# Head mixing attention: a block's values made behind the scores two tiles on, and VectorE's copy of the outputs behind the next maxima and running sum

## What is computed

```python
attn = jnp.einsum('bhnd,bhmd->bhnm', q, k) * scale
attn = jax.nn.softmax(attn, axis=-1)
attn = jnp.einsum('gh,bhnm->bgnm', conv_w, attn) + conv_b[None, :, None, None]
mean = attn.mean(axis=(0, 2, 3), keepdims=True)
var = attn.var(axis=(0, 2, 3), keepdims=True)
attn = (attn - mean) * jax.lax.rsqrt(var + BN_EPS)
attn = attn * bn_gamma[None, :, None, None] + bn_beta[None, :, None, None]
out = jnp.einsum('bhnm,bhmd->bhnd', attn, v)
```

## Time and profile before

| | |
|---|---|
| median of 3 runs | 4358.7 us (4358.68 to 4359.67) |
| the profiled execution's own time | 4354.42 us |
| its span, first to last instruction | 4352.6 us |
| busy over the span: TensorE, VectorE, ScalarE, GpSimd | 87%, 64%, 51%, 19% |
| busy in one block of 35.15 us in the middle of the stage: TensorE, VectorE, ScalarE, GpSimd | 34.07, 30.58, 26.15, 6.84 us |
| share of the chain that ended last that lies in this stage's lines | none of the lines listed |

### The profile page before, as it was taken

One profiled execution on the slowest core, in us unless ns is written; L12 is line 12 of the kernel. 1 busy time (PEld: TensorE's weight loads), 2 busy tenths in 40 slices (PEclk: granted clock), 3 DMA queues, 4 the chain that ended last, 5 costly groups with the idle time before them and its releaser, 6 DMA issues. The chain is left out here.

```text
span 4352.6 us, 155594 instructions
## 1 busy us (share of the span) xinstructions
PE 3782.2 (87%) x64620; PEld 2304.4 (53%) x64621; DVE 2787.5 (64%) x5455; ACT 2209.1 (51%) x4201; POOL 825.7 (19%) x2119
## 2 busy tenths in 40 slices
PE   5779999799799997688889759999999999966996
PEld 2357777444477774345555425445545545434763
DVE  5546666311566664578788658878878878863343
ACT  1235555311455552466666527767767767721221
POOL 0000000000000000355555401111111111105023
PEclk7879999899899997899999879999999999988997
DMA  1011111100011111000000021000000000023233
GB/s 52 10 32 48 48 51 50 35 0 0 26 48 48 51 49 62 1 1 1 1 1 1 1 74 35 0 1 1 0 1 1 0 1 0 0 90 116 64 92 113
DMA packets 84608, 131.16 MB, mean 30 GB/s; under 512 B 11440, under 2 KB 67024, under 8 KB 83408
## 3 DMA queue, kind: packets, MB, share of 16 engines
q1 hardware_dynamic: 78288, 111.95, 7.7%
q0 software_dynamic: 6144, 16.79, 1.2%
HBM read 69.98 MB, written 58.72 MB: 30 GB/s over the span
## 5 line engine op out<-in xcount | busy, mean ns | idle before, releaser
L1969 PE MATMUL psum<-hm_ex,hm_mix 128*128 128x512 f32 x1024 | 503.0, 614 | 38.8 <-ACT hm_Aq L2065 38.8
L2051 ACT ACTIVATE hm_ex<-psum,hm_nm 128x1024 f32<-128x1024 f32 x256 | 286.0, 1117 | 255.5 <-DVE hm_nm L2123 255.3
L1969 PEld LDWEIGHTS psum<-hm_ex,hm_mix 128*128 128x128 f32 x1024 | 173.9, 189 | 344.8 <-issue 336.9
L2138 DVE COPY hm_A<-psum 128x1024 f32<-128x1024 f32 x256 | 312.7, 1222 | 54.0 <-PE psum L1978 50.3
L2133 DVE TENSOR_SCALAR_CACHE_REDUCE hm_plus<-hm_Aq,hm_cbcol,hm_sums 128x1024 f32<-128x1024 f32 x256 | 340.3, 1329 | 0.0
L2123 DVE TENSOR_REDUCE hm_nm<-psum 128x1 f32<-128x1024 f32 x256 | 310.7, 1214 | 32.2 <-PE psum L1957 32.2
L1978 PEld LDWEIGHTS psum<-K,hm_Aq 128*128 128x128 f32 x2048 | 236.7, 141 | 149.4 <-issue 139.7
L1529 ACT ACTIVATE pt_signs<-pt_acts,pt_tb 128x1024 f32<-128x1024 f32 (+1 forms) x224 | 227.6, 1018 | 116.0 <-POOL pt_tb L1399 94.9
L2056 ACT ACTIVATE hm_junk<-hm_Aq 128x1024 f32<-128x1024 f32 x256 | 270.6, 1057 | 30.3
L1957 PE MATMUL psum<-hm_kt,hm_qd 64*32 64x512 f32 x4096 | 277.9, 601 | 3.2 <-ACT hm_kt L2074 3.2
L1978 PE MATMUL psum<-K,hm_Aq 128*128 128x128 f32 x2048 | 267.3, 273 | 5.6 <-DVE hm_A L2138 5.6
(11 more groups left out here) (415 smaller groups left out, 7949.7 us busy)
## 6 DMA issues: line engine op xcount, KB each, us to landing
fw_late<-fw_away SPq DMA_DIRECT2D x64, 384.0 KB, 3.1
ex_rows_in<-hm_zero SPq DMA_DIRECT2D x2, 5120.0 KB, 24.2
ex_xs<-ex_rows_in SPq DMA_DIRECT2D x80, 128.0 KB, 2.0
ex_rows_out<-ex_ys SPq DMA_DIRECT2D x80, 128.0 KB, 1.7
fw_away<-fw_kk SPq DMA_DIRECT2D x64, 128.0 KB, 1.8
fw_away<-fw_tr SPq DMA_DIRECT2D x64, 128.0 KB, 1.7
fw_away<-fw_qm SPq DMA_DIRECT2D x64, 128.0 KB, 1.7
ex_w<-in_ex_w SPq DMA_DIRECT2D x2, 4096.0 KB, 19.6
```

Of the source, the lines that this page charges most:

```text
L1969: mm = pe.matmul(bank[4 + c], mix[:, u, :], ex[:, u, 512 * c:512 * c + 512], start=True, stop=True)
L2051: act.activation(ex[:, u, :], flat2(psum[:, 2 * u:2 * u + 2, :]), ACT.Exp, bias=nm[:, u:u + 1], accum_out=rsum[:, u:u + 1]).then_inc(s_ex, 1)
L2138: dve.tensor_copy(A[:, :, :, QT_ * t:QT_ * t + QT_], flat2(psum[:, 6:8, :]).rearrange("p (m g n) -> p m g n", m=MT, g=HEADS)).then_inc(s_a ...
```

## The change

In every block but a batch's first, at tiles 1 and 2:

- TensorE, tile 1: `scores` of tile 3 goes ahead of `values`, and `turn` of tile 0, which closed tile 1, leaves it.
- TensorE, tile 2: after `mixed` of 2 come the wait for `outputs`, `turn` of 0, `scores` of 4 and `turn` of 1 (before: `turn` of 1, `scores` of 4).
- VectorE, tile 1: `maxima` of 3 and `running` of 1 go ahead of `outputs` and `evacuate` of 0; tile 2 is left with `inverse` of 3 and `evacuate` of 1.

No instruction is added or removed, and no buffer changes.

```diff
                             mixed(i, t % 2, more)
                             if t == 0 and not first:
                                 turn(i - 1, 1)
+                            if t > 2 or t == 2 and first:
+                                turn(i - 1, (t - 1) % 2)
+                            if t == 2 and not first:
+                                pe.wait_ge(s_pv_ev, b * NB * 2 + n * 2 + 2)
+                                turn(i - 2, 0)
+                            if more:
+                                scores(i + 2, t % 2)
+                            if t == 1 and first:
+                                pe.wait_ge(s_v_ev, b * 2 + 2)
+                                turn(i - 1, 0, free=False)
                             if t == 1 and not first:
                                 values(n - 1)
-                            if t > 1:
-                                turn(i - 1, (t - 1) % 2)
-                            if more:
-                                scores(i + 2, t % 2)
-                            if t == 1:
-                                if first:
-                                    pe.wait_ge(s_v_ev, b * 2 + 2)
-                                else:
-                                    pe.wait_ge(s_pv_ev, b * NB * 2 + n * 2 + 2)
-                                turn(i - 1, 0, free=not first)
+                            if t == 2 and not first:
+                                turn(i - 1, 1)
...
                             more = not (last and t == NQ - 1 or first and t == 0)
-                            if more:
+                            early = t == 2 and not first
+                            if more and not early:
                                 maxima(i + 1, (t + 1) % 2)
-                            if not (first and t == 0):
+                            if not (first and t == 0) and not early:
                                 running(i - 1, (t - 1) % 2)
                             if more:
                                 inverse(i + 1, (t + 1) % 2)
                             if t == 1 and not first:
+                                maxima(i + 2, t % 2)
+                                running(i, t % 2)
                                 outputs(n - 1)
                             if not (first and t == 0):
                                 evacuate(i - 1, (t - 1) % NQ)
```

## The result

| | before | the change |
|---|---|---|
| median | 4359.48 us (12 runs, 4352.26 to 4370.03) | 4377.89 us (12 runs, 4367.28 to 4384.18) |
| ratio | | 1.0033, interval 1.0025 to 1.0041 |
| span of the profiled execution | 4352.6 us | 4376.4 us |
| a block in the middle of the stage | 35.15 us | 35.59 us |

A forecast was written before the change was run, and what follows sets the result against it. TensorE was taken to set the pace, standing 1.08 us a block; a new chain of waits adds 0.38 us at each of 28 boundaries, 10.6 us, to 4358.7, giving 4369.3 us. Range 4358 to 4380 us, the forecast's own 4363 to 4376.

The forecast's parts named there:

- the three cases: Whole program against a 0.2% threshold: slower by more 0.61, faster by more 0.10, between 0.29.
- rival 3: Boundary: longer `mixed` of 2 (1.91) and bank release (1.52) cost 0.7 us each, 19.6 us in all, 4378 us; chance 0.09.
- the forecast's chain: Boundary, banks 6 and 7: linked waits from `mixed` of 1 bring `mixed` of 4 at 2737.95 instead of 2737.55, 0.40 us later.
- What bounds: Within a block TensorE sets the pace, 3.81 us a tile; its only stand is 1.08 us ahead of `mixed` of 3.
- rival 1: Boundary: early maxima free `keep`, nothing replaces the 1.08 us wait; 30.2 us faster, 4328.5 us; chance 0.09.
- What goes: Boundary: `maxima` of 3 and `running` of 1 fit VectorE's 2.92 us idle gap, ending the old reason for the 1.08 us.
- The two waits: TensorE at a boundary: about 0.5 us ahead of `turn` of 1 and 1.0 us ahead of `mixed` of 4.
- VectorE's four gaps: Idle at a boundary: 0.3 ahead of `maxima`, 1.2 of `outputs`, 2.1 of `evacuate` of 0, 1.15 of `evacuate` of 1.
- the signs of being wrong: `mixed` of 4 under 16.1 us behind `mixed` of 1, a block's tile pace other than 3.81 us, or TensorE clock below 1.00.
- `mixed` of 2 to `turn` of 0: TensorE at a boundary, start to start: 1.76 us taken, from 1.72 or 1.79 in the trace, bound 1.91.
- The sum: All 28 boundaries at 0.38 us each: 10.6 us slower; batch ends, first blocks and other stages cost nothing more.
- Rival 2: Within the block: the delay is caught up over five tiles, no measurable change, 4354 to 4364 us; chance 0.22.

The follow-up runs named there:

- the last experiment: Kernel before, only `maxima` of 3 moved on VectorE, behind `outputs` and ahead of `evacuate` of 0 at every boundary; TensorE's order unchanged: ratio 0.9929.
- TensorE's half alone: TensorE's order as in the change, VectorE's as in the kernel before: ratio 1.021.
- VectorE's half alone: VectorE's order as in the change, TensorE's as in the kernel before: ratio 1.0227, from two runs.
- with `turn` of 0 back: Against the change: wait for `outputs` and `turn` of 0 back ahead of `mixed` of 2, `turn` of 1 ahead of `scores` of 4; VectorE as changed: ratio 0.9984.

## Why the prediction was right

The measured median, 4377.89 us, lies in the range, near its upper end; slower by over 0.2% was the likeliest of the three cases and came. It lies outside the forecast's own 4363 to 4376 us, though, and right at rival 3's 4378: by the time alone rival 3 would have come. That the forecast's chain is what happened is told by the trace, with 0.44 us a boundary and not 0.7. By its steps:

- **What bounds.** Right. TensorE stood 1.08 us a block, and nothing else could be gained: the version that removes exactly that reaches 34.10 us and the 30 us that rival 1 had reckoned for it.
- **What goes.** Right as to `maxima` of 3 (2735.28, 0.23 us behind the reciprocal), its `exponentials` and the early `keep` of 2, released by `turn` of 0.
- **The chain.** Right in every link, most of them to 0.02 us: 1.91, 1.02, 3.63, then 1.82, 1.08, 1.37, 1.10, 1.14, 1.25, 1.11 and 1.15. Together 16.58 us from `mixed` of 1 to `mixed` of 4, where I had 16.52 and the kernel before has 16.12. The two waits are 0.39 and 1.08 us where I had 0.5 and 1.0, and VectorE's four gaps 0.23, 1.23, 2.15 and 1.18 where I had 0.3, 1.2, 2.1 and 1.15. Of the signs of being wrong none came at a boundary; a clock below 1.00 came once, at the stage's last `values`.
- **The term that was mis-sized** is `mixed` of 2 to `turn` of 0: 1.76 taken, 1.82 measured, just outside the 1.72 and 1.79 between which I chose, though inside the bound of 1.91. The weight loads of that `mixed` started with its first matmul, at 2738.73 for both, and not ahead of it:

```profile
2738.73 0.30 PEld L1970 LDWEIGHTS psum<-hm_ex,hm_mix 128*128 128x128 f32 x2 [0.20 <-issue]
```

The Trainium skill's rule of weight loads pulled ahead (TensorE: Matmul & The Clock Gate, the table of facts at its head) is not what happened at this place, although `weights` of tile 2 had long been done; by it the sum would have been 0.34 us a boundary, by the trace it is 0.44. The trace of before had held the right figure: in its ordinary tiles, where `mixed` follows `scores`, the first weights start with the matmul and `turn` comes 1.83 us behind.

```profile
2737.55 1.98 PE L1969 MATMUL psum<-hm_ex,hm_mix 128*128 128x512 f32 x4
2739.38 1.04 PE L1978 MATMUL psum<-K,hm_Aq 128*128 128x128 f32 x8
```
```profile
2737.55 0.30 PEld L1969 LDWEIGHTS psum<-hm_ex,hm_mix 128*128 128x128 f32 x2 [0.84 <-issue]
```
- **The sum.** 28 x 0.38 = 10.6 us forecast; 28 x 0.44 = 12.3 us in the trace; 14.4 us by the ratio, whose interval of 10.9 to 17.9 holds 12.3. The remaining 1.3 us that the profiled stage is longer is the clock at its last `values`, to which the prediction ("the batch ends ... cost nothing more") gave nothing. Whether the change brought that fall is open: each kernel has one profile. My point of 4369.3 us is 8.6 below the median, of which the chain explains 1.7; the rest is within what runs of one kernel differ by.
- **Rival 1** (faster, the wait goes and nothing replaces it) did not come, for the reason given. Its price was right, and its place was one step away: with `maxima` of 4 taken forward too it is at 34.47 us, with TensorE left alone at 34.10. What I had written under it as needed was too little: since a boundary starts from a loss of 0.40 us, half of the gain (0.54) asks for a chain shorter by 0.94 us and not by 0.7, and all of it for 1.48 and not 1.0.
- **Rival 2** (caught up within the block) did not come: behind the wait the tiles take 3.78 us (2748.75 to 2752.53) and no less. **Rival 3** (0.7 us a boundary) did not either.
- The advice of the Trainium skill that rival 1 names (Perfetto Trace Analysis, Optimization Strategy: find the gap and make what it waits for start sooner) agrees with the last experiment (34.10 us a block) and not with the change (35.59). Both make the same maxima sooner; they differ in what they make later.

## What to carry to other kernels

When a step is moved forward on an in-order engine to end a wait, follow the next instance of the same step too: it may now be queued behind something that waits longer, and the old wait comes back one tile on. An idle gap on a helping engine is best filled with just what the bound engine waits for and what fits the gap; here one 1.2 us step moved gained 31 us, while moving two steps there and reordering three on TensorE lost 14. Before reordering the bound engine, look whether a reorder on the engine that it waits for is enough.

## What the hardware showed that was not expected

TensorE's clock fell at block boundaries only where it stood longer. With stands of up to 1.12 us the granted clock was 1.00 in the blocks read of the kernel before, of the change and of the four variants other than its halves. In TensorE's half alone it stood 2.22 us ahead of `mixed` of 3, and in VectorE's half alone 3.04 or 3.12 us ahead of `turn` of 0; at 23 and at 19 of the 28 boundaries the matmuls behind the stand then ran slow, at 0.50 to 0.52 where the clock was read, the level of 1.2 GHz. In TensorE's half that cost 1.7 us in the block shown (38.62 against 36.92) and up to 3.0 in others (39.9). The two stands of 2.22 us shown above are equal and only one was followed by the fall. Directly ahead of both TensorE had run the same steps at the same distances, with the 0.39 us ahead of `turn` of 1, and the block before each was a slow one (38.5 and 38.62 us). What decides between the two was not settled. At the end of the stage the clock fell behind shorter stands. The last `values` follows stands of 1.41 and 1.3 us, with one `turn` between them, in all eight profiles. It took 3.70 us in the kernel before, in the maxima alone, in TensorE's half and with `turn` of 0 back, and 5.05 to 5.37 us in the change and the other three. In the 14 us ahead of it TensorE's steps lie at the same distances before and in the change; what decides is open here too. The forecast's bare remark that the new stands are no longer than the old holds for the change's 28 boundaries, where the clock is 1.00, and would not have held for either half.
